# A two-block graph transformer on one core: maxima split on GpSimd, half of the masks there, q stored six times, new slots, and a last batch in the score banks

## The chip, the cores and the metric

The kernel runs on one core of one Trainium2 chip. The metric is the device time of one execution in microseconds, the median of several runs. TensorE (PE in the profile; PEld is its weight loading), VectorE (DVE), ScalarE (ACT), GpSimd (POOL) and SyncE (SP, which only issues DMAs here) each work through a queue of their own, in order, and wait for each other on semaphores.

## The reference, cut to what matters

```
x: (16, 512, 128)   adj: (512, 512) bool, symmetric, with the diagonal
h = relu(layernorm(x))
q, k, v = split(h @ W_qkv + b_qkv)                    # 8 heads of 16
attn = softmax(where(adj, q k^T / sqrt(16), -inf))    # per batch and head: 512 x 512
x = x + (attn v) @ W_out + b_out
h = relu(layernorm(x))
zl, zg, v = h @ Wl, h @ Wg, h @ Wv
A_l = max(cosine(zl, zl), 0),  A_g = exp(-|zg_i - zg_j|^2 / 2)   # both times adj, with the diagonal 0
K = 0.9 A_l / rowsum(A_l) + 0.1 A_g / rowsum(A_g)     # row sums floored at 1e-8
x = x + (K v) @ Wo
```

## The kernel before, in words

All 16 batches go through one software pipeline. Time is counted in **slots**, 32 to a batch. In slot u of a batch TensorE makes one 128x512 tile of scores (`scores`, L595; 8 heads x 4 row tiles), and VectorE adds the mask and reduces its row maxima in one instruction (L820). 21 slots later (`LAG`) TensorE makes the same scores a second time, turned (`turned_scores`, L608 and L609): keys on partitions, queries along the free axis. This product has 96 rows of q and k and three more, which subtract the maximum. ScalarE takes the exp (L979). Every four slots `attend` (L623) multiplies four tiles by v.

**Exactness.** q and k are split into three bf16 parts (hi, mid, lo), and the six important products of parts are six groups of 16 rows (`Q_PARTS`, `K_PARTS`): 96 rows. To get there, the parts are stored to DRAM (`split_dram`, L441, six DMAs of 128 KB: from SBUF's 128 partitions, 8 heads outermost in the destination) and loaded again in row order for each half of the heads (L410: six DMAs per half, three of them for q broadcasts of one stored part). The maxima of a half are split in three bf16 parts on VectorE (`max_split`, L828 to L835), turned on TensorE (`max_turn`, L689), copied by ScalarE (L1004) and loaded as three rows (L426). Other products split their float32 operands in two parts and make three matmuls (`split_product`, L630).

**Masks.** A turned tile is masked in one of two ways: TensorE adds a mask matrix to the bank ahead of the scores (L608; for w % 4 in `MASK_BY_PE` = 1, 2, 3, 24 tiles per batch), or GpSimd multiplies the exp's result by an integer mask (L485, the other 8), one slot after.

**The second block** of a batch works in the slots 62 to 99 after its first score, so beside the next two batches' attention. ScalarE copies z = h W (`z_copy`) and sums its squares (`z_sums`, L1057). GpSimd makes the norms (`z_norms`, L551 to L562) and divides zl by them. TensorE turns zg, zl and a bias (L641), makes four 128x512 tiles of the cosine and four of the rbf adjacency in one bank each (`adj_bank`), VectorE masks them (L843, L852, L857), and `mix` (L635) multiplies them by v. VectorE divides by the row sums (`out`, L863 to L874). The transposes, q, k, v, the maxima and the projection share one PSUM bank, `work_bank`; before a stage writes it, TensorE waits for the reader of the stage before (`bank_free`, `BANK_READ`).

**What sets the order** is the table `AT`: for each stage its slots counted from the first score of its batch. Every engine runs the same loop over slots and issues what `due` says is due, within a slot in the order in which the code has it. The slots set only the order in each queue; times follow from the waits. A stage at slot 78 of batch b stands in the queue where batch b + 2 is in its slot 14. `rows` and `qk_store` are negative: -16 is slot 16 of the batch before.

```
    "ln_rstd": (-33,), "q_split": (-24,), "k_split": (-18,), "x_biased": (-13,), "ln2_rstd": (61,),
    "qk_store": (-16,), "rows": (-11, -9), "x_next": (-14,), "max_load": (17, 33), "store": (98,),
```

The set-up turns the adjacency into masks on TensorE, ScalarE and VectorE, and GpSimd fills 32 rows of `qk_rows` with ones (L546, 6.9 us).

Of the kernel before, what the change touches and what calls it, by code (L numbers as in the profile page):

```python
# [5 lines left out]
F32 = mybir.dt.float32  # L6
F32R = mybir.dt.float32r
BF16 = mybir.dt.bfloat16
# [4 lines left out]
P = 128  # L13
# [7 lines left out]

Q_PARTS = (0, 0, 0, 1, 1, 2)
K_PARTS = (0, 1, 2, 0, 1, 0)
Q_RUNS = ((0, 3), (1, 2), (2, 1))
# [8 lines left out]
MASK_BY_PE = (1, 2, 3)  # L33
# [4 lines left out]
    "hT": (-26,), "q": (-24,), "k": (-22,), "v": (-15,), "max_turn": (16, 32),  # L38
    "pv": (28, 32, 36, 40, 44, 48, 52, 56), "y": (54, 59), "yT": (61,), "attn": (62,), "h2T": (67,),
    "z": (69, 70, 72, 73), "zgT": (76,), "col": (78,), "zlT": (79,), "rbf": (79, 83, 85, 87),  # L40
    "cos": (81, 83, 87, 89), "mix_cos": (93, 94, 96, 98), "mix_rbf": (94, 95, 96, 98),

    "ln_scale": (-28,), "hT_copy": (-26,), "q_hi": (-24,), "k_hi": (-22,), "max_copy": (15, 32),
    "pv_copy": (40, 57), "yT_copy": (60,), "ln2_scale": (64,), "h2T_hi": (67,), "z_copy": (69, 70, 72, 74),
    "z_sums": (70, 73, 74, 75), "zgT_hi": (75,), "col_copy": (77,), "zlT_hi": (78,), "rbf_exp": (82, 83, 85, 87),

    "ln_moments": (-35,), "hT_split": (-26,), "q_rest": (-24,), "k_rest": (-21,), "v_add": (-13,),
    "max_split": (15, 32), "y_scale": (55, 60), "x1": (62,), "ln2_moments": (62,), "h2T_lo": (67,),
    "zgT_lo": (76,), "zlT_lo": (79,), "rbf_read": (79, 83, 85, 87), "cos_read": (81, 83, 87, 91),
# [8 lines left out]
LAST = max(max(at) for at in AT.values()) + 1  # L58
# [14 lines left out]
def graph_blocks(nc, x, adj, w_qkv, b_qkv, w_out, b_out, w_l, w_g, w_v, w_o, out):  # L73
# [10 lines left out]
    ZC = 3 * D + 2  # L84
# [4 lines left out]

    def due(slot, name):  # L90

        for nth, at in enumerate(AT[name]):
            batch, rest = divmod(slot - at, SLOTS)
            if rest == 0 and 0 <= batch < B:
                return batch, nth
        return None
# [7 lines left out]
    with ExitStack() as ctx:  # L104
# [25 lines left out]
        bar_bias = sb("bar_bias", [P, 1])  # L130
        table_warm = sb("table_warm", [P, T])
        degree_floor = sb("degree_floor", [P, 2])
# [46 lines left out]
        inv_norm = sb("inv_norm", [P, T])  # L179
        rbf_bias = sb("rbf_bias", [P, T])  # L180
        zl_unit = sb("zl_unit", [P, T, D])
# [16 lines left out]
        split_dram = nc.dram_tensor("split_dram", (2, 3, DH, H, N), BF16, kind="Internal").ap()  # L198
# [15 lines left out]
        s_row_ones = signal("setup_row_ones")  # L214
# [36 lines left out]
        split_stored = [signal(f"split_stored{which}", 3, 16) for which in range(2)]  # L251
        rows_loaded = [signal(f"rows_loaded{h}", len(Q_RUNS) + len(K_RUNS), 16) for h in range(GROUPS)]
# [41 lines left out]
        unit_ready = signal("unit_ready")  # L294
# [19 lines left out]
        out_stored = signal("out_stored", 1, 16)  # L314

# [784 lines left out]
```

## Time and profile before

| | us |
|---|---|
| median of three runs | 914.6 (914.2 to 916.01) |
| the profiled execution | 914.57 |
| its span, first to last instruction | 912.8 |
| TensorE busy | 829.5 |
| VectorE busy | 718.8 |
| ScalarE busy | 532.2 |
| GpSimd busy | 348.7 |

The span is one execution's, from its first to its last instruction; the execution's own time is 1.8 us more. Busy times are sums over instructions, and busy TensorE is modelled at the ends of matmuls. Some matmul records are missing from the trace (307 of the 384 mask matmuls are in it).

### The profile page before, as it was taken

What the parts mean: (1) busy time and instruction counts of PE and PEld (TensorE: products, weight loads), DVE (VectorE), ACT (ScalarE), POOL (GpSimd) and SP (SyncE); (2) the same over time, 40 slices, a digit from 0 to 9 for tenths busy, and PEclk for the clock granted to TensorE, in tenths of its full rate; (3) what the DMA queues carried; (4) which work ended last, traced back from release to release, by engine and by line L of the source; (5) the groups of instructions that cost most, each with busy time, mean ns of one, the idle gap of its engine ahead of it and who ended that gap; (6) DMA issues with size and microseconds to landing.
All of it is one profiled execution on the core that took longest, in us unless ns stands there. A gap on an engine that the chain in (4) does not pass through costs nothing.

```text
span 912.8 us, 15340 instructions
## 1 busy us (share of the span) xinstructions
PE 829.5 (91%) x4870; PEld 482.8 (53%) x4947; DVE 718.8 (79%) x2078; ACT 532.2 (58%) x1226; POOL 348.7 (38%) x415
## 2 busy tenths in 40 slices
PE   3388899999999999999999999999999999999976
PEld 2133346546464646546564655646465554646455
DVE  5677879797887978798887979788797879786434
ACT  4136675856556575755647585655657575565630
POOL 5334452533435352443534253353525244233210
PEclk9569999999999999999999999999999999999987
DMA  3231313130311213030211213031121303000000
GB/s 98 69 104 43 88 36 82 29 94 24 86 39 47 72 37 92 27 87 30 68 50 48 83 29 91 23 89 39 40 77 34 97 21 88 23 1 13 1 12 12
DMA packets 43423, 48.45 MB, mean 53 GB/s; under 512 B 6992, under 2 KB 37200, under 8 KB 43344
## 3 DMA queue, kind: packets, MB, share of 16 engines
q1 hardware_dynamic: 43344, 47.47, 19.1%
q8 instruction: 41, 0.67, 0.3%
q14 instruction: 38, 0.31, 0.1%
HBM read 30.28 MB, written 16.78 MB: 52 GB/s over the span
## 4 chain that ended last, share of the span: by engine, by line
PE 78%; DVE 11%; issue 4%; DMA 3%; ACT 2%; POOL 1%; SPq 1%; DVEq 0%; ACTq 0%; POOLq 0%
PE adj L630 13%; PE adj L635 12%; PE pv L623 12%; PE score L595 12%; PE turned L609 12%; PE turned L608 6%; PE work L641 5%; PE work L630 3%; DVE scrap L820 3%; DMA qk_rows<-split_dram 2%; PE work L712 1%; PE work L730 1%; DVE rbf_arg L852 1%; DVE zgT_parts L947 1%; DVE max_parts L828 1%
## 5 line engine op out<-in xcount | busy, mean ns | idle before, releaser
L820 DVE CUSTOM_DVE_ANT_0 scrap<-score,mask_add 128x512 f32<-128x512 f32 x512 | 337.8, 684 | 49.3 <-PE score L595 45.6
L979 ACT ACTIVATE probs_t<-turned 128x512 f32<-128x512 f32 x512 | 293.3, 595 | 130.3 <-PE turned L609 127.6
L485 POOL TENSOR_TENSOR probs_t<-probs_t,keep_t 128x512 int32<-128x512 int32 x128 | 170.3, 1331 | 258.9 <-ACT probs_t L979 258.9
L595 PE MATMUL score<-qk_rows 96*128 96x512 bf16 x512 | 202.0, 396 | 18.0 <-DMA qk_rows<-split_dram 14.4
L609 PE MATMUL turned<-qk_rows 99*128 99x512 bf16 x512 | 195.3, 381 | 6.4 <-DVE zgT_parts L947 1.9
L623 PE MATMUL pv<-probs_t,v_cols 128*32 128x512 f32 x1024 | 136.4, 605 | 0.0
L608 PE MATMUL turned<-bar_t,ident_b 128*128 128x512 bf16 x307 | 117.4, 382 | 7.3 <-ACT probs_t L979 7.3
L595 PEld LDWEIGHTS score<-qk_rows 96*128 96x128 bf16 x512 | 50.0, 98 | 127.4 <-issue 77.7
L1013 ACT ACTIVATE rbf_exp<-rbf_arg,rbf_bias 128x512 f32<-128x512 f32 x64 | 46.1, 721 | 65.4 <-DVE rbf_arg L852 65.4
L609 PEld LDWEIGHTS turned<-qk_rows 99*128 99x128 bf16 x512 | 50.6, 99 | 44.3 <-issue 1.0
L635 PEld LDWEIGHTS adj<-z,adj_cos 128*128 128x128 f32 x512 | 66.5, 190 | 11.7 <-DVE adj_cos L843 2.1
L630 PE MATMUL adj<-zlT_parts 128*128 128x512 f32 x192 | 68.5, 466 | 2.2 <-DVE zlT_parts L952 1.4
L635 PE MATMUL adj<-z,adj_cos 128*128 128x130 f32 x512 | 67.8, 275 | 2.4 <-DVE adj_cos L843 1.4
L635 PE MATMUL adj<-z,adj_rbf 128*128 128x130 f32 x512 | 67.4, 275 | 0.0
L635 PEld LDWEIGHTS adj<-z,adj_rbf 128*128 128x128 f32 x512 | 63.2, 191 | 2.1
L630 PE MATMUL adj<-zgT_parts 128*128 128x512 f32 x192 | 63.2, 439 | 0.8 <-DVE rbf_arg L852 0.8
L523 POOL TENSOR_SCALAR var_eps<-moments 128x4 f32<-128x4 f32 x16 | 3.9, 241 | 149.1 <-DVE moments L803 149.1
L843 DVE SCALAR_TENSOR_TENSOR adj_cos<-adj,mask_t 128x512 f32<-128x512 f32 x64 | 44.0, 688 | 14.6 <-PE adj L630 14.5
L608 PEld LDWEIGHTS turned<-bar_t,ident_b 128*128 128x128 bf16 x384 | 38.1, 99 | 31.3 <-ACT probs_t L979 18.5
L630 PE MATMUL adj<-wz_parts,h2T_parts 128*128 128x384 f32 x192 | 52.4, 386 | 1.4 <-DVE h2T_parts L942 1.4
L515 POOL CAST split<-resid 128x512 bf16<-128x512 f32 x31 | 19.0, 611 | 85.8 <-DVE resid L896 85.8
L852 DVE TENSOR_TENSOR rbf_arg<-adj,col_term 128x512 f32<-128x512 f32 x64 | 43.8, 684 | 7.6 <-PE adj L630 7.6
(123 smaller groups left out, 1206.7 us busy)
## 6 DMA issues: line engine op xcount, KB each, us to landing
split_dram<-split SPq DMA_DIRECT2D x96, 128.0 KB
qk_rows<-split_dram SPq DMA_DIRECT2D x64, 192.0 KB
qk_rows<-split_dram SPq DMA_DIRECT2D x64, 128.0 KB
x_sb<-in_x_dram SPq DMA_DIRECT2D x16, 256.0 KB, 2.9
qk_rows<-split_dram SPq DMA_DIRECT2D x64, 64.0 KB
out_dram<-out_sb SPq DMA_DIRECT2D x16, 256.0 KB, 2.3
qk_rows<-max_rows SPq DMA_DIRECT2D x96, 4.0 KB, 1.7
adj_sb<-in_adj_dram SPq DMA_DIRECT2D x1, 256.0 KB, 2.9
```

The lines of the kernel that those rows point to most:

```text
L485: pool.tensor_tensor(tile, tile, keep_t[:, w // HG % T, :], ALU.mult).then_inc(probs_masked.sem, 1)
L595: pe.matmul(score_bank[u % 2][:, :], qk_rows[0:ROWS, b % 2, 0, h, t * P:(t + 1) * P], qk_rows[0:ROWS, b % 2, 1, h, :], start=True, stop=Tr ...
L608: pe.matmul(turned_bank[w % 2][:, :], ident_b[:, :], bar_t[:, j, :], start=True, stop=False)
L609: pe.matmul(turned_bank[w % 2][:, :], qk_rows[0:ROWS + 3, b % 2, 1, h, j * P:(j + 1) * P], qk_rows[0:ROWS + 3, b % 2, 0, h, :], start=w no ...
L623: last = pe.matmul(pv_bank[32 * hl:32 * (hl + 1), :], v_cols[:, b % 3, j, g * HG + hl, :], probs_t[:, k % 4, hl, :], start=(j == 0), stop= ...
L630: last = pe.matmul(dst, left(a), right(c), start=(part == 0), stop=(part == 2))
L635: last = pe.matmul(adj_bank[n % 2][:, at:at + D + 2], adjacency[:, m, n * P:(n + 1) * P], z[:, m, 2 * D:ZC], start=(m == 0), stop=(m == T ...
L641: last = pe.transpose(work_bank[:, t * P:(t + 1) * P], src(t), ident[:, :])
L820: dve.tensor_tensor_reduce(scrap[:, u % 2, :], score_bank[u % 2][:, :], mask_add[:, u % T, :], -1.0, 3.0e38, ALU.add, ALU.min, neg_max[:, ...
L852: dve.tensor_tensor(rbf_arg[:, m % 2, :], adj_bank[1][:, :], col_term[:, :], ALU.add).then_inc(rbf_arg_ready.sem, 1)
L979: act.activation(probs_t[:, k % 4, w % HG, :], turned_bank[w % 2][:, :], ACT.Exp, scale=SCALE).then_inc(probs_ready.sem, 1)
L1013: act.activation(rbf_exp[:, m % 2, :], rbf_arg[:, m % 2, :], ACT.Exp, bias=rbf_bias[:, m:m + 1]).then_inc(rbf_exp_ready.sem, 1)
```

## The change

- **Masks.** `MASK_BY_PE` is (2, 3): TensorE adds the mask for 16 tiles a batch, GpSimd multiplies 16.
- **Maxima.** The four steps of `max_split` move from VectorE's queue to GpSimd's; half 0 is turned in slot 17.
- **h.** ScalarE writes the first part of hT straight from the bank, then the copy; VectorE takes the rest from the bank too, without its cast (L884).
- **q and k.** q is stored six times, one for each group of rows, k three times: nine DMAs per batch; each half loads q in one DMA and k in three. The fill of ones is made by ScalarE in four activations.
- **Second block.** zl is turned without being divided; v is divided by the norm instead (`v_cos`), and the floor of the degree is scaled by it. z products wait for the second part of h only at their third matmul. A row of z has one column of constants, 129 columns are mixed for 130.
- **Idle matmuls.** 20 at set-up, and one in each of the slots 0 to 20, write a bank that nobody reads then.
- **Slots.** `AT` has new numbers throughout. Batches 14 and 15 have tables of their own (`AT_BEFORE_LAST`, `AT_LAST`). Batch 15 uses the four score and turned banks for z and for mixing, and `pv_bank` and `work_bank` as second banks of the cosine and rbf tiles; its squares are summed on VectorE; each row block is mixed into all four banks as it comes; the output is made step by step over four blocks and stored in four DMAs.

```diff
-MASK_BY_PE = (1, 2, 3)
+MASK_BY_PE = (2, 3)
+IDLE_SET_UP = 20
+IDLE_FIRST_SLOTS = range(0, LAG)
...
-    "qk_store": (-16,), "rows": (-11, -9), "x_next": (-14,), "max_load": (17, 33), "store": (98,),
+    "qk_store": (-12,), "rows": (-6, -4), "x_next": (-9,), "max_load": (-2, 29), "store": (95,),
...
+                            if which:
+                                places = [k_dram[part]]
+                            else:
+                                places = [q_dram[c] for c, p in enumerate(Q_PARTS) if p == part]
+                            for place in places:
+                                sp.dma_start(place.rearrange("f h n -> h f n"),
+                                             split[:, which, part, :]).then_inc(split_stored[which].sem, 16)
...
+                sp.dma_start(qk_rows[0:ROWS, batch % 2, 0, heads, :],
+                             q_dram[:, :, heads, :].rearrange("c f h n -> (c f) (h n)")
...
+                if hit := due(s, "max_split"):
+                    b, g = hit
+                    reached(pool, max_ready, b, (g + 1) * HALF)
+                    reached(pool, max_turned, b - 1, g + 1)
+                    pool.tensor_copy(max_parts[:, g, 0, :], neg_max[:, g, :]).then_inc(max_hi.sem, 1)
...
+                pe.wait_ge(s_mask_add.sem, 1)
+
+                reached(pe, hi_ready, 0, 2)
+                reached(pe, rest_ready, 0, 2)
+                idle(IDLE_SET_UP)
...
-                    reached(act, hT_split, b - 1)
+                    reached(act, qk_filled, b - 1)
+                    act.copy(hT_parts[:, 0, :], work_bank[:, :]).then_inc(hT_hi.sem, 1)
                     act.copy(hT[:, :], work_bank[:, :]).then_inc(hT_ready.sem, 1)
...
+                    pool.tensor_tensor(v_cos[:, :, 0:D], z[:, :, 2 * D:3 * D],
+                                       v_cos[:, :, D:D + 1].broadcast_to([P, T, D]),
+                                       ALU.mult).then_inc(v_cos_ready.sem, 1)
...
+        def z_bank(batch, t):
+            return (score_bank + turned_bank)[t] if batch == B - 1 else adj_bank[t % 2]
+        def cos_bank(batch, m):
+            return pv_bank if batch == B - 1 and m % 2 else adj_bank[0]
+        def rbf_bank(batch, m):
+            return work_bank if batch == B - 1 and m % 2 else adj_bank[1]
+        def mix_bank(batch, n):
+            return (score_bank + turned_bank)[n] if batch == B - 1 else adj_bank[n % 2]
```

**GpSimd's queue, one middle batch, slots 8 to 20.** `probs_t` rows are masks, `split` rows the parts of q and then k, `norm_floor` to the row with `z` the norms. Before:

```order
L515 CAST split<-resid 128x512 [waits rest_ready,split_stored0]
L517 TENSOR_TENSOR split<-resid,split 128x512 [waits mid_ready]
L485 TENSOR_TENSOR probs_t<-probs_t,keep_t 128x512 [waits probs_ready]
L551 TENSOR_SCALAR norm_floor<-square_sum 128x4 [waits sums_ready]
L555 TENSOR_SCALAR rbf_bias<-square_sum 128x4 [waits col_filled,rbf_exp_ready]
L558 TENSOR_TENSOR inv_norm<-norm_floor,minus_half 128x4 [waits floor_ready]
L562 TENSOR_TENSOR zl_unit<-z,inv_norm 128x512 [waits zlT_filled,inv_norm_ready]
L485 TENSOR_TENSOR probs_t<-probs_t,keep_t 128x512 [waits probs_ready]
L515 CAST split<-resid 128x512 [waits rest_ready,split_stored1]
L517 TENSOR_TENSOR split<-resid,split 128x512 [waits mid_ready]
L485 TENSOR_TENSOR probs_t<-probs_t,keep_t 128x512 [waits probs_ready]
```

and now:

```order
L625 TENSOR_SCALAR norm_floor<-square_sum 128x4
L629 TENSOR_TENSOR v_cos<-norm_floor,minus_half 128x4 [waits mix_filled,floor_ready]
L632 TENSOR_TENSOR v_cos<-z,v_cos 128x4x128 [waits inv_norm_ready]
L635 TENSOR_TENSOR norm<-norm_floor,v_cos 128x4
L639 TENSOR_SCALAR degree_floor<-norm 128x4 [waits out_ready,norm_ready]
L585 CAST max_parts<-neg_max 128x16 [waits max_turned,max_ready]
L587 TENSOR_TENSOR max_rest<-neg_max,max_parts 128x16 [waits max_hi]
L590 CAST max_parts<-max_rest 128x16 [waits max_rest_ready]
L592 TENSOR_TENSOR max_parts<-max_rest,max_parts 128x16 [waits max_mid]
L547 TENSOR_TENSOR probs_t<-probs_t,keep_t 128x512 [waits probs_ready] x4
L615 TENSOR_TENSOR x_resid<-x_sb,bias_out 128x512 [waits x1_ready,x_loaded]
L577 CAST split<-resid 128x512 [waits rest_ready,k_stored]
```

The four steps on `max_parts` now stand behind the norms and ahead of four masks, and the parts of k behind all of these.

**SyncE's queue from the maxima to the rows of the next batch's half 0.** Before:

```order
L453 DMA out_dram<-out_sb 128x4x128 [waits out_ready]
L441 DMA split_dram<-split 8x16x512 [waits hi_ready,rows_loaded1,rows_loaded0]
L441 DMA split_dram<-split 8x16x512 [waits hi_ready]
L441 DMA split_dram<-split 8x16x512 [waits mid_ready] x2
L441 DMA split_dram<-split 8x16x512 [waits lo_ready] x2
L426 DMA qk_rows<-max_rows 1x16x128 [waits turned_filled,max_copied]
L426 DMA qk_rows<-max_rows 1x16x128 x2
L377 DMA x_sb<-in_x_dram 128x4x128 [waits x_resid_ready,ln_done]
L410 DMA qk_rows<-split_dram 48x1x2048 [waits turned_filled,split_stored1,split_stored0]
L410 DMA qk_rows<-split_dram 48x2048
L410 DMA qk_rows<-split_dram 32x1x2048
```

and now, where the first six loads of maxima are half 1 of one batch and half 0 of the next:

```order
L477 DMA qk_rows<-max_rows 1x16x128 [waits turned_filled,max_copied]
L477 DMA qk_rows<-max_rows 1x16x128 x2
L510 DMA out_dram<-out_sb 128x4x128 [waits out_ready]
L497 DMA q_dram<-split 8x16x512 [waits hi_ready,rows_loaded1,rows_loaded0]
L497 DMA q_dram<-split 8x16x512 x2
L497 DMA k_dram<-split 8x16x512 [waits hi_ready]
L497 DMA q_dram<-split 8x16x512 [waits mid_ready]
L497 DMA q_dram<-split 8x16x512
L497 DMA k_dram<-split 8x16x512 [waits mid_ready]
L497 DMA q_dram<-split 8x16x512 [waits lo_ready]
L497 DMA k_dram<-split 8x16x512 [waits lo_ready]
L430 DMA x_sb<-in_x_dram 128x4x128 [waits x_resid_ready,ln_done]
```

The stores were ahead of the loads of half 0's maxima and are behind them now; after the last store only x stands ahead of the rows, whose first load (96x2048) follows it.

**TensorE's queue in the last batch, from z's transposes on.** Before, with one bank for each kind of tile and zl behind the bias:

```order
L641 MATMUL work<-ident,z 128x128 [waits h2T_split,z_ready]
L641 MATMUL work<-ident,z 128x128 x3
L641 MATMUL work<-ident,rbf_bias 128x128 [waits zgT_split,rbf_bias_ready]
L641 MATMUL work<-ident,rbf_bias 128x128 x3
L630 MATMUL adj<-zgT_parts 128x512 [waits z_ready,zgT_split]
L630 MATMUL adj<-zgT_parts 128x512 x2
L641 MATMUL work<-ident,zl_unit 128x128 [waits col_ready,unit_ready]
L641 MATMUL work<-ident,zl_unit 128x128 x3
L630 MATMUL adj<-zlT_parts 128x512 [waits z_ready,zlT_split]
L630 MATMUL adj<-zlT_parts 128x512 x2
L630 MATMUL adj<-zlT_parts 128x512 [waits cos_ready]
L630 MATMUL adj<-zlT_parts 128x512 x2
```

and now, with `pv` and `work` as second banks:

```order
L740 MATMUL work<-ident,z 128x128 [waits h2T_split,z_ready]
L740 MATMUL work<-ident,z 128x128 x3
L740 MATMUL pv<-ident,z 128x128 [waits pv_copied,z_ready]
L740 MATMUL pv<-ident,z 128x128 x3
L717 MATMUL adj<-zgT_parts 128x512 [waits out_ready,zgT_split]
L717 MATMUL adj<-zgT_parts 128x512 x2
L717 MATMUL adj<-zlT_parts 128x512 [waits out_ready,zlT_split]
L717 MATMUL adj<-zlT_parts 128x512 x2
L740 MATMUL work<-ident,rbf_bias 128x128 [waits zgT_split,rbf_bias_ready]
L740 MATMUL work<-ident,rbf_bias 128x128 x3
L717 MATMUL pv<-zlT_parts 128x512 x3
L717 MATMUL adj<-zlT_parts 128x512 [waits cos_ready]
```

The transposes of zl stand right behind those of zg and wait for no norm.

## Rows read from the trace of the kernel before

**Rows 1.** The page, busy shares and clock row.
```profile
PE 829.5 (91%) x4870; PEld 482.8 (53%) x4947; DVE 718.8 (79%) x2078; ACT 532.2 (58%) x1226; POOL 348.7 (38%) x415
...
PEclk9569999999999999999999999999999999999987
```

**Rows 2.** Windows: us, busy (x) PE, PEld, DVE, ACT, POOL, PEclk, DMA share, GB/s.
```profile
310.27:362.47 52.20, 50.02 (x305) 29.66 (x310) 44.03 (x130) 32.67 (x77) 21.13 (x25) 1.00 0.21 55
18.00:20.00 2.00, 0.00 (x0) 0.00 (x0) 2.00 (x3) 2.00 (x5) 2.00 (x2) 1.00 0.49 151
28.00:30.00 2.00, 0.00 (x0) 0.00 (x0) 1.66 (x9) 0.00 (x0) 0.16 (x1) 0.50 1.02 164
880.00:900.00 20.00, 14.24 (x41) 9.19 (x39) 7.79 (x12) 7.20 (x26) 2.50 (x4) 0.62 0.00 0
```

**Rows 3.** Timeline of TensorE in one middle batch.
```profile
314.33 0.38 PE L595 MATMUL score<-qk_rows 96*128 96x512 bf16 x1
...
342.54 0.22 PE L689 MATMUL work<-ident_b,max_parts 128*48 128x128 bf16 x1 [1.37 <-DVE zlT_parts L952]
...
353.69 0.38 PE L608 MATMUL turned<-bar_t,ident_b 128*128 128x512 bf16 x1
353.91 0.38 PE L609 MATMUL turned<-qk_rows 99*128 99x512 bf16 x1
```

**Rows 4.** Waits of TensorE, 310.27 to 362.47: us, times, longest.
```profile
PE work L689 <- DVE zlT_parts L952: 1.4, 1, 1.4
PE turned L608 <- ACT probs_t L979: 0.5, 1, 0.5
```

**Rows 5.** Groups by form: busy us, mean ns | idle before.
```profile
L820 DVE CUSTOM_DVE_ANT_0 scrap<-score,mask_add 128x512 f32<-128x512 f32 x512 | 337.8, 684 | 49.3 <-PE score L595 45.6
...
L1057 ACT ACTIVATE adj_cos<-z 128x128 f32<-128x128 f32 x128 | 38.9, 314 | 0.0
...
L835 DVE TENSOR_TENSOR max_parts<-max_rest,max_parts 128x16 bf16<-128x16 f32 x32 | 18.4, 574 | 1.1
...
L558 POOL TENSOR_TENSOR inv_norm<-norm_floor,minus_half 128x4 f32<-128x4 f32 x16 | 16.6, 1036 | 0.0
...
L1028 ACT COPY hT<-work 128x512 f32<-128x512 f32 x16 | 9.4, 585 | 8.5 <-PE work L641 8.5
...
L523 POOL TENSOR_SCALAR var_eps<-moments 128x4 f32<-128x4 f32 x16 | 3.9, 241 | 149.1 <-DVE moments L803 149.1
```

**Rows 6.** Single lines: min/median/max ns.
```profile
L857 DVE SCALAR_TENSOR_TENSOR adj_rbf<-rbf_exp,mask_t x64: 680/686/1190, 140.5 to 900.7; 128x512 f32<-128x512 f32 x64
...
L485 POOL TENSOR_TENSOR probs_t<-probs_t,keep_t x128: 1266/1277/1770, 59.7 to 856.1; 128x512 int32<-128x512 int32 x128
```

**Rows 7.** Timeline of SyncE's queue, start and middle.
```profile
15.41 4.22 SPq L441 DMA_DIRECT2D split_dram<-split  x6
...
319.03 1.82 SPq L426 DMA_DIRECT2D qk_rows<-max_rows  x3
```

**Rows 8.** The start: chain of work and TensorE's timeline.
```profile
19.07 3.21 DMA split_dram<-split
...
34.99 1.01 PE L595 MATMUL score<-qk_rows 96*128 96x512 bf16 x2 [12.57 <-DMA qk_rows<-split_dram]
...
53.23 0.30 PE L689 MATMUL work<-ident_b,max_parts 128*48 128x128 bf16 x1 [1.18 <-DVE max_parts L835]
...
69.43 0.38 PE L595 MATMUL score<-qk_rows 96*128 96x512 bf16 x1 [1.04 <-DVE neg_max L820]
...
89.61 0.24 PE L689 MATMUL work<-ident_b,max_parts 128*48 128x128 bf16 x1 [0.79 <-DVE max_parts L835]
...
107.69 0.39 PE L595 MATMUL score<-qk_rows 96*128 96x512 bf16 x1 [1.82 <-DMA qk_rows<-split_dram]
```

**Rows 9.** TensorE's timeline, the last batch.
```profile
888.57 1.65 PE L630 MATMUL adj<-zlT_parts 128*128 128x512 f32 x3 [1.40 <-DVE zlT_parts L952]
...
900.96 2.02 PE L635 MATMUL adj<-z,adj_cos 128*128 128x130 f32 x16 [1.38 <-DVE adj_cos L843]
```

More of the change, by code:

```diff
@@ L88, in graph_blocks, with slots_of @@
     by_pool = [w for w in range(SLOTS) if w % HG not in MASK_BY_PE]
-    def due(slot, name):
[L92 to L96, printed above, removed]
+    def slots_of(name, batch):
+        table = {B - 1: AT_LAST, B - 2: AT_BEFORE_LAST}.get(batch, AT)
+        return [at + SLOTS * batch for at in table.get(name, AT[name])]
+    stages = {}
+    for name in AT:
+        for batch in range(B):
+            for nth, at in enumerate(slots_of(name, batch)):
+                assert (at, name) not in stages
+                stages[at, name] = batch, nth
+    def due(slot, name):
+        return stages.get((slot, name))
     def tile_due(slot, lag):
@@ L568, in _, with idle @@
             pe.wait_ge(s_ident.sem, 1)
+            def idle(times):
+                for _ in range(times):
+                    pe.matmul(pv_bank[:, :], ident_b[:, :], mask_add[:, 0, :], start=True, stop=True)
             def turn_masks(blocks):
@@ L626, in attend, with split_product, mix, v_of_cos @@
                 last.then_inc(pv_filled.sem, 1)
-            def split_product(dst, left, right):
+            def split_product(dst, left, right, before_rest=None):
                 for part, (a, c) in enumerate(((0, 0), (0, 1), (1, 0))):
+                    if part == 2 and before_rest:
+                        before_rest()
                     last = pe.matmul(dst, left(a), right(c), start=(part == 0), stop=(part == 2))
                 return last
-            def mix(n, at, adjacency):
-                for m in range(T):
-                    last = pe.matmul(adj_bank[n % 2][:, at:at + D + 2], adjacency[:, m, n * P:(n + 1) * P],
-                                     z[:, m, 2 * D:ZC], start=(m == 0), stop=(m == T - 1))
-                return last
-            def turn_tiles(src, ready):
+            def mix(bank_, adjacency, n, right, rows):
+                for m in rows:
+                    last = pe.matmul(bank_, adjacency[:, m, n * P:(n + 1) * P], right(m), start=(m == 0),
+                                     stop=(m == T - 1))
+                return last
+            def v_of_cos(m):
+                return v_cos[:, m, :]
+            def v_of_rbf(m):
+                return z[:, m, 2 * D:ZC]
+            def cos_half(batch, n):
+                return mix_bank(batch, n)[:, 0:D + 1]
+            def rbf_half(batch, n):
+                return mix_bank(batch, n)[:, 256:256 + D + 1]
+            def turn_tiles(src, ready, bank_=work_bank):
                 for t in range(T):
-                    last = pe.transpose(work_bank[:, t * P:(t + 1) * P], src(t), ident[:, :])
+                    last = pe.transpose(bank_[:, t * P:(t + 1) * P], src(t), ident[:, :])
                 last.then_inc(ready.sem, 1)
@@ L868, in _ @@
[L868 to L875 removed]
+                    blocks = [n] if b < B - 1 else range(T)
@@ L959, in _, with fill_ones @@
             act.activation(table_warm[:, :], minus_half[:, :], ACT.Exp)
+            def fill_ones():
+                act.wait_ge(s_mask_add.sem, 1)
+                for half in range(GROUPS):
+                    for place in range(2):
+                        act.activation(qk_rows[ROWS:P, place, 1, half * HG:(half + 1) * HG, :],
+                                       mask_add[ROWS:P, :, :], ACT.Identity, bias=one[ROWS:P, 0:1],
+                                       scale=0.0).then_inc(s_row_ones.sem, 1)
             def cast_masks():
```

307 lines of the change are left out of this document (186 added, 121 removed).

## Prediction

> **What bounds the kernel now.** First the page's busy shares: TensorE 91% of the span, next VectorE 79% [rows 1]. A share is a mean over stages, so I cut one period out of the middle, 310.27 to 362.47, 52.2 us from a mixing step to the same one a batch later. In it TensorE is busy 50.0 us, VectorE 44.0, ScalarE 32.7, GpSimd 21.1 [rows 2]. Ends of matmuls are modelled, so I checked by starts: from a mask matmul's start to the next one's, 353.69 to 353.91, is 0.22 us [rows 3], and that is the distance nearly everywhere. What is left are two waits, 1.4 us before the transposed maxima (TensorE needs the work bank, which VectorE frees late) and 0.5 us behind ScalarE's exp [rows 4]. So the middle is bound by TensorE. The ends are not: the first score starts at 34.99, after 12.6 us of waiting for the rows of q and k [rows 8]; the clock row stands at half until 62 us and dips again near the end [rows 1]; and at the end the last batch runs alone through a chain of small steps, its first cosine product at 888.57 and its mixing from 900.96 [rows 9].
>
> **The middle: 13 batches (2 to 14).** Eight of the 24 mask matmuls per batch go: 8 x 0.22 = 1.76 us, all on the path, since TensorE is packed. GpSimd gets eight more masks of 1.28 us (10.2 us, from the median in [rows 6]), the eight small steps of the maxima (0.24 us each, 1.9 us) and two small ones in place of none [rows 5]: 21.1 + 10.2 + 1.9 + 0.5 = 33.7 of 50 us. A pair's masks are due four or more slots later (6 us) and take 2.6, so they lie beside other work. Of small GpSimd steps there are two prices in the trace, 0.24 us (add, multiply) and 1.04 us (power) [rows 5]. No row shows a 16-element split on GpSimd; I take 0.24, since it is a cast and a subtraction like the nearest row, and keep 1.04 for the range.
>
> VectorE loses the split of the maxima (its last step alone 0.57 us, twice a batch [rows 5]) and the cast of h, so it has under 43 of 50 us to do: nothing directly. But the 1.4 us wait was just this: the split stood in slot 15 ahead of the step that frees the bank [rows 4]. With the split gone and the turn one slot later, it goes: 1.4 us. What is late next is ScalarE. Slots 4 to 11 are its densest (a layer norm, eight squares of 0.31 us and their read-outs [rows 5], the copies of z, q and k), and TensorE stalls 0.5 us behind it. There it gets one copy more (0.585 us [rows 5]) and TensorE arrives 0.44 us earlier (two mask matmuls less): +1.0 us. Sum per batch: -1.76 - 1.4 + 1.0 = -2.2, a period of 50.0 us, and 13 x 2.2 = **28.6 us**. Norms that multiply v and not zl, one column less in the mixing and the new slots otherwise I cost at nothing: they exchange like for like inside GpSimd's 16 idle us and TensorE's queue. A misplaced slot would show as a new wait, between 0 and 1.5 us per batch (the largest one here is 1.4).
>
> **GpSimd beside VectorE.** The mask of the second adjacency on VectorE reads two SBUF tiles; it takes 686 ns at the median and up to 1190 [rows 6], so at most 0.5 us each, 2 us per batch on an engine with 7 us to spare. I take nothing, and 2 us for the range. The Trainium skill (SBUF — State Buffer, "Who interferes with whom") says that a VectorE instruction with two SBUF inputs is blocked by a GpSimd one that reads SBUF, for the whole instruction. By it twice the masks mean twice the collisions, which speaks against the change; an estimate from it and the mask's length would be up to 1.28 us for each of four steps, 5 us per batch. The row's longest excess, 0.5 us, agrees in kind and is far smaller.
>
> **The rows of q and k.** Now q is stored six times, so nine stores per batch where there were six, and they start only after the maxima of half 0 are loaded (SyncE's queue: turn, three loads, the output's store, then the nine). Six stores took from 15.41 to their landing at 22.28 [rows 7, 8], 6.9 us for 0.79 MB; the busiest window shows 151 GB/s with 0.49 of 16 engines [rows 2], so 5.2 us of data and 1.7 of the rest. Nine: 7.8 + 1.7 = 9.5 us, though the queue issues them in 5.2. The loads of half 0 bring 0.79 MB; at 164 GB/s, seen with all engines busy [rows 2], 4.8 us, with 1.2 to land 6.0. Before, the loads of half 0 took from about 22.3 to 34.7, 12.4 us [rows 8]. The skill (DMA: Bandwidth & Descriptors, "Why a DMA increments its semaphore by 16 and not by 1") says that a transfer uses the largest number of engines, at most 16, that divides the outermost size of both sides: three or two for the old broadcasts, all for the new loads, but eight for every store. By this rule the trace agrees: 0.49 of 16 is eight.
> In the middle this loop is: first score to turn, 28.2 before [rows 3], less four mask matmuls (0.9) and the 1.4 wait, with ScalarE's 1.0 and one slot's score, turned score and cosine product (1.3): 28.2. Then copy 0.3, three loads 1.8 [rows 7], output store 0.4, stores 9.5, x 0.5, loads 6.0, and 1.4 for the bytes of x and output in the same engines: 48.1 us, against a period of 50.0. Hidden, with 1.9 us to spare.
>
> **The start.** Stores from 15.5: 25.0, then x 0.2, loads 6.0: first score at 31.2 in place of 34.99. GpSimd's long fill of ones (7 us) moves to ScalarE, which idles there. Twenty idle matmuls (at 0.43 us, half clock, 8.6 us) lie inside TensorE's wait for rows and end by 31. One more in each of the first 21 slots lies under VectorE's 0.70 us per score (0.684 and a read-out [rows 5]). They are to hold the clock; if not, TensorE needs two times 0.43 per slot, 0.16 more than VectorE, 3 us. But the loop binds here, since early slots are short: batch 0 reaches the turn in 17.4 us (18.2 before, 34.99 to 53.23 [rows 8], less 1.5 for the clock and the split, plus a slot of 0.7) and batch 1 in 19.7 (20.2 before, 69.43 to 89.61 [rows 8], less 0.9 for mask matmuls and 0.8 of waiting, plus a slot of 1.2); each adds 0.3 + 1.8 + 9.5 + 0.5 + 6.0. So 31.2 + 35.5 + 37.8 = 104.5 for batch 2's first score, before 107.69 [rows 8]: **3.2 us** (0 to 8, the upper end if stores overlap better).
>
> **The end.** After batch 15's first score 13 mask matmuls fewer: **2.9 us**. Then the lone batch. Its projection and h2T come 1.4 us sooner, as its turn of y no longer waits behind mixing. The products of z go to four banks, start on the first part of h, and the squares leave ScalarE, where they delayed the z copies and the cast behind them (eight, 0.31 us each and a read-out), while zl's transposes no longer wait for the norms on GpSimd. I get the first cosine product 5.7 us sooner than 888.57 [rows 9]. From there to the end of the span the old chain takes 24.2 us: single banks, all mixing after 900.96, four outputs in turn. The new one has two banks each, and mixes row by row: eight VectorE reads and four masks in 10.8 us, the last four products 0.9, the four outputs step by step 3.8, the store 2.4: 17.9, so 6.3 saved. These are full-clock numbers; the row shows 0.62 there [rows 2], so I give back 2.5. **9.5 us** (5 to 12).
>
> **Sum.** The profiled execution took 914.57 us (span 912.8, 1.8 around it; median of the runs 914.6). 28.6 + 3.2 + 2.9 + 9.5 = 44.2, so **870.4 us**.
>
> **The rivals.**
> *The loop of rows binds in every batch.* If its true length is over 50, TensorE waits at each first score. For it: a margin of 1.9 us on a sum of eight terms, and two waits for rows at the start [rows 8]. Against: in the middle no wait for rows is in the list today [rows 4], and the new loads spread better. At 51.1 us (my sum short by 3): 13 x 1.1 + 15.6 = 29.9, 884.7 us.
> *All waits vanish.* The slots fit, and ScalarE's wait goes too: 50.0 - 1.76 = 48.3, just above the loop: 13 x 3.9 + 15.6, 848.3 us. Against: ScalarE's dense stretch is still there.
> *GpSimd becomes the bound, and it is slower.* All is in one queue in order: at the upper prices (small steps 1.04, masks 1.77 [rows 6]) its sum is 33.7 + 6.4 + 7.8 = 48 us, and it must wait some 6 us for square sums and for the last reduction before each split, with masks, the k split and stores queued behind. A period of 54.0: 13 x 1.8 longer, less 15.6, 922.4 us. It decides from 53.4 us per batch. Against: both upper prices are rare in the trace.
> *No effect:* TensorE only seems packed and another bound holds the middle near 53. Spacing of 0.22 between starts speaks against it.
>
> **Chances.** Forecast (860 to 880) 0.62, loop of rows 0.22, no waits 0.09, GpSimd 0.05, no effect 0.02. Two ends of unknown costs (start 3 to 5, end 4, new waits up to 13 x 0.7) and most of the loop's case give 854 to 889. Faster by over 0.2% (what a measurement of this kernel can tell) 0.93, within it 0.02, slower 0.05.
>
> **What would show it.** Mask matmuls 256 in place of 384, mean start spacing in the middle 50.0 us; the wait of the transposed maxima on VectorE gone, the one on exp near 1.5; GpSimd near 34 us per batch with small casts of 0.24; stores of nine in about 9.5 us; no wait for rows after batch 2; first score near 31; clock 1.0 from about 30 us on; 18 us from the first cosine product of batch 15 to the end. A wait of score matmuls on the row loads in each batch would make the loop right, one of pv on GpSimd's masks the third rival.

## The result, and the profile after

| | before | after | forecast |
|---|---|---|---|
| median, us | 914.4 (912.8 to 916.0) | 875.67 (872.3 to 875.9) | 870.4 (854 to 889) |
| ratio, 95% interval | | 0.9568 (0.9539 to 0.9596) | 0.952 |
| span of the profiled execution | 912.8 | 870.6 | 868.6 |
| first score of batch 0 | 34.99 | 30.41 | 31.2 |
| first score of batch 2 | 107.69 | 103.71 | 104.5 |
| first score of batch 15 | 784.41 | 755.16 | |
| steady period (batches 3 to 14) | 52.23 | 50.14 | 50.0 |

The traced execution of after is the shortest of its four (span 870.6 at a mean clock of 0.988). The other three, without a trace, took 873.9 to 874.1 at 0.983 to 0.986, so what they lost is not seen, only that they had more half clock.

The page's shares (columns as in [rows 1]) and one steady period by windows (columns as in [rows 2]):

```profile
PE 814.5 (94%) x4860; PEld 467.4 (54%) x4860; DVE 674.6 (77%) x1950; ACT 544.3 (63%) x1230; POOL 532.0 (61%) x701
...
PEclk9899899999999999999999999999999999999999
```

```profile
60.00:64.00 4.00, 1.32 (x5) 0.44 (x6) 1.56 (x6) 0.60 (x1) 2.06 (x6) 0.67 0.99 251
64.00:68.00 4.00, 4.00 (x15) 0.76 (x14) 1.06 (x3) 0.75 (x2) 1.66 (x4) 0.50 0.30 65
100.00:104.00 4.00, 1.11 (x4) 0.34 (x5) 3.17 (x15) 0.60 (x1) 1.50 (x8) 0.79 1.00 247
104.00:108.00 4.00, 4.00 (x14) 0.75 (x13) 0.85 (x3) 0.69 (x3) 3.69 (x6) 0.50 0.42 89
303.88:354.06 50.18, 49.25 (x303) 28.86 (x300) 41.67 (x120) 33.19 (x77) 33.03 (x44) 1.00 0.25 67
840.00:860.00 20.00, 17.41 (x118) 15.44 (x118) 14.44 (x52) 7.69 (x15) 4.60 (x10) 1.00 0.05 14
```

In the period GpSimd is busy 33.0 us, as forecast (33.7). The clock is full at the end (0.62 there before [rows 2]), but at half, 1.2 GHz, from 61.3 to 68.3 and from 102.3 to 109.3. Ahead of the first stands a wait of 4.02 us behind VectorE, and at both a wait for rows (TensorE's timeline):

```profile
60.40 0.39 PE L680 MATMUL score<-qk_rows 96*128 96x512 bf16 x1 [4.02 <-DVE neg_max L955]
...
63.50 0.61 PE L680 MATMUL score<-qk_rows 96*128 96x512 bf16 x1 [2.28 <-DMA qk_rows<-k_dram]
...
103.71 0.61 PE L680 MATMUL score<-qk_rows 96*128 96x512 bf16 x1 [2.64 <-DMA qk_rows<-k_dram]
...
852.85 0.40 PE L717 MATMUL adj<-zlT_parts 128*128 128x512 f32 x1
```

The last line is batch 15's first cosine product, 17.75 us ahead of the end (forecast 17.9). The waits of TensorE in the steady period, 303.88 to 354.06 (us, times, longest):

```profile
PE turned L694 <- ACT probs_t L1126: 0.6, 1, 0.6
PE adj L717 <- DVE rbf_arg L983: 0.4, 1, 0.4
```

The wait of the turned maxima [rows 4] is gone. A new one stands at the bank of the rbf tile, behind VectorE. Why VectorE is late there is seen when its timeline and GpSimd's are laid side by side. After, VectorE, then GpSimd:

```profile
334.72 1.71 DVE L988 SCALAR_TENSOR_TENSOR adj_rbf<-rbf_exp,mask_t 128x512 f32<-128x512 f32 x1
...
337.56 1.12 DVE L988 SCALAR_TENSOR_TENSOR adj_rbf<-rbf_exp,mask_t 128x512 f32<-128x512 f32 x1
```
```profile
334.58 1.30 POOL L615 TENSOR_TENSOR x_resid<-x_sb,bias_out 128x512 f32<-128x512 f32 x1
335.81 1.09 POOL L577 CAST split<-resid 128x512 bf16<-128x512 f32 x1
336.98 1.16 POOL L579 TENSOR_TENSOR split<-resid,split 128x512 bf16<-128x512 f32 x1
```

L988 takes 0.686 us at the median. At 334.72 it begins just behind GpSimd's addition, which ends at 335.88, and ends at 336.43, 0.55 after that. At 337.56 it begins inside a subtraction that ends at 338.14, and ends at 338.68, 0.54 after it. So it stands until GpSimd's instruction is over. The period's other two have no GpSimd instruction beside them and take 0.68 and 0.69. GpSimd waits in its turn: its cast is 1.09 long at 335.81 and 0.62 at the median. The Trainium skill (SBUF — State Buffer, "Who interferes with whom") says that whichever of the two engines issues first has the shared access to SBUF for its whole instruction, and that a VectorE instruction with two inputs in SBUF needs it beside a GpSimd instruction that reads SBUF. The trace agrees: 1.71 and 1.12 us for 0.686. The mask of the cosine tile reads one input from PSUM, and never takes over 0.692 us in this trace.

**Where the time came from**, profiled executions: up to batch 2's first score 4.0 us; from there to batch 15's 25.3 (676.7 before, 651.4 after); from there to the end 13.0; together 42.2 before rounding.

### The profile page after: what moved, and what is told of

The parts are those of the page before. It is cut to its first block, busy times and chain, and to the rows that moved or that the text cites. A ratio compares the mean times of both kernels' runs of the same rounds, so it can differ in the third digit from the quotient of the medians.

```text
span 870.6 us, 15444 instructions
## 1 busy us (share of the span) xinstructions
PE 814.5 (94%) x4860; PEld 467.4 (54%) x4860; DVE 674.6 (77%) x1950; ACT 544.3 (63%) x1230; POOL 532.0 (61%) x701
## 4 chain that ended last, share of the span: by engine, by line
PE 54%; DVE 16%; POOL 11%; issue 7%; ACT 6%; DMA 3%; SPq 2%; POOLq 0%; DVEq 0%; ACTq 0%
PE adj L722 12%; PE pv L708 9%; PE score L680 7%; PE turned L694 7%; DVE scrap L955 6%; PE adj L717 6%; PE work L740 4%; PE turned L693 4%; POOL probs_t L547 3%; DVE adj_cos L974 3%; DVE adj_rbf L988 3%; DVE rbf_arg L983 2%; PE work L717 2%; POOL v_cos L632 2%; POOL v_cos L629 2%
## 5 line engine op out<-in xcount | busy, mean ns | idle before, releaser
L547 POOL TENSOR_TENSOR probs_t<-probs_t,keep_t 128x512 int32<-128x512 int32 x256 | 322.4, 1280 | 213.4 <-ACT probs_t L1126 213.1
L693 PE MATMUL turned<-bar_t,ident_b 128*128 128x512 bf16 x256 | 98.0, 383 | 0.7 <-ACT probs_t L1126 0.7
L722 PEld LDWEIGHTS adj<-v_cos,adj_cos 128*128 128x128 f32 x480 | 62.8, 191 | 8.8 <-DVE out_sb L1011 0.6
L717 PE MATMUL adj<-zlT_parts 128*128 128x512 f32 x186 | 64.3, 454 | 0.1
L988 DVE SCALAR_TENSOR_TENSOR adj_rbf<-rbf_exp,mask_t 128x512 f32<-128x512 f32 x64 | 63.0, 985 | 1.2 <-ACT rbf_exp L1160 1.2
L722 PE MATMUL adj<-v_cos,adj_cos 128*128 128x129 f32 x480 | 63.4, 274 | 0.4 <-DVE out_sb L1011 0.4
L722 PE MATMUL adj<-z,adj_rbf 128*128 128x129 f32 x480 | 63.2, 275 | 0.0
L1151 ACT COPY max_rows<-work 48x128 bf16<-48x128 bf16 x32 | 8.2, 258 | 86.2 <-PE work L815 86.2
L717 PEld LDWEIGHTS adj<-zgT_parts 128*128 128x128 f32 x186 | 33.9, 189 | 22.4 <-DVE rbf_arg L983 11.9
L708 PEld LDWEIGHTS pv<-probs_t,v_cols 128*32 128x32 f32 x1024 | 20.3, 108 | 45.8 <-issue 29.2
L974 DVE SCALAR_TENSOR_TENSOR adj_cos<-adj,mask_t 128x512 f32<-128x512 f32 x62 | 42.5, 686 | 2.3 <-PE adj L717 2.3
```

What stands on the lines that cost most here:

```text
L547: pool.tensor_tensor(tile, tile, keep_t[:, w // HG % T, :], ALU.mult).then_inc(probs_masked.sem, 1)
L693: pe.matmul(turned_bank[w % 2][:, :], ident_b[:, :], bar_t[:, j, :], start=True, stop=False)
L708: last = pe.matmul(pv_bank[32 * hl:32 * (hl + 1), :], v_cols[:, b % 3, j, g * HG + hl, :], probs_t[:, k % 4, hl, :], start=(j == 0), stop= ...
L717: last = pe.matmul(dst, left(a), right(c), start=(part == 0), stop=(part == 2))
L722: last = pe.matmul(bank_, adjacency[:, m, n * P:(n + 1) * P], right(m), start=(m == 0), stop=(m == T - 1))
L974: dve.scalar_tensor_tensor(adj_cos[:, m, :], cos_bank(b, m)[:, :], 0.0, mask_t[:, m, :], ALU.max, ALU.mult).then_inc(cos_ready.sem, 1)
```

## Experiments: how many masks on GpSimd

Three kernels are the one after with another number of masks on TensorE: (1, 2, 3) in m24_pe, shown here, (3,) in m8_pe, and none in m0_pe. One, before_m16, is the kernel before with the change's (2, 3) alone.

```diff
-MASK_BY_PE = (2, 3)
+MASK_BY_PE = (1, 2, 3)
```

> The changed kernel with eight masks per batch put back on TensorE (24 of 32 there). Mine, TensorE packed: each mask matmul is worth its start spacing of 0.22 us, so the steady period goes from 50.14 to 51.9 us and the time from 872.3 to about 896 (1.76 x 13.5 batches). Rival, something else sets 50.14 (GpSimd's queue, slots, VectorE): less than a third of that, period under 50.7 and time under 880. The mask on VectorE that runs beside GpSimd's masks (985 ns mean now, 772 before the change) should fall towards 772.

> The changed kernel with eight more masks per batch on GpSimd (24 there, 8 on TensorE). TensorE packed and nothing else: period 48.4, time 849. Rival, GpSimd's queue in order becomes late: its busy time is 33.0 + 10.2 = 43.3 of 48.4 us, so the parts of the maxima and the masks come late; period 50 to 52 and a time of 872 to 895, with waits of pv on GpSimd's masks or of the turned maxima on their last part. I hold the rival's lower half likelier: 868 to 880, since three of four tiles would then be masked in one stretch of 7.7 us every 12.

> The changed kernel with all 32 masks on GpSimd, none on TensorE. GpSimd's busy time would be 33.0 + 20.5 = 53.5 us per batch, above the 50.14 of now. If busy time binds: period at least 53.5, time at least 872.3 + 13 x 3.4 = 916, the third rival of the prediction made real. If TensorE alone counted: period 46.6, time 826. The VectorE mask beside it should rise above 985 ns at the mean.

> The kernel before with the masks of the change alone (16 on TensorE). Mine, the term for masks in the sum: 8 x 0.22 = 1.76 us per batch, so about 914.4 - 1.76 x 13.5 = 890.6 us, and the wait of the transposed maxima for the work bank stays at 1.4 or grows. Rival, TensorE only arrives earlier at that wait and at the one on exp: half the gain or less, 903 and over.

| masks on TensorE | kernel | time | ratio to before | period | GpSimd busy in it | mean of VectorE's mask, ns |
|---|---|---|---|---|---|---|
| 24 | after | 885.1 | 0.9661 (0.9627 to 0.9696) | 50.93 | 22.8 | 806 |
| 16 | after | 875.7 | 0.9568 (0.9539 to 0.9596) | 50.14 | 33.0 | 985 |
| 8 | after | 899.6 | 0.9816 (0.978 to 0.9851) | 52.3 | 43.7 | 1274 |
| 0 | after | 975.4 | 1.0642 (1.0597 to 1.0686) | 56.6 | 53.9 | 1421 |
| 24 | before | 914.4 | 1 | 52.23 | 21.1 | 772 |
| 16 | before | 924.7 | 1.0091 (1.0067 to 1.0115) | 52.9 | 31.1 | 773 |

(The periods of the irregular kernels are means over 11 batches; the 43.7 is from a period of 51.62.) **Eight masks were worth 0.79 us a period, not 1.76.** Both theories of the first run miss. Laying one steady period of TensorE of m24_pe beside one of after, instruction by instruction, tells why: at each of the eight places TensorE gains 0.22 us, and elsewhere it gives 0.97 back. The largest step, +0.72, is the first product of an rbf tile at 340.55; the rest are steps of 0.08 and 0.09 around the exp and at transposes. In m24_pe the wait for the rbf tile's bank is not there:

```profile
PE turned L693 <- ACT probs_t L1126: 0.5, 1, 0.5
```

The price of a mask matmul was right, but what stood behind it was not free. (m24_pe keeps the slots that were chosen for 16 masks; no others were tried for it.)

**With 8 or none on TensorE** it is slower than either of my theories had it (899.6 for at most 895, and 975.4 for 916 or more), and before GpSimd is full: at 8 it is busy 43.7 of 51.6 us. Its norms come late in its queue, behind the masks, and TensorE waits for them, in m8_pe 13 times over the whole kernel; with none pv waits for the masks themselves, in m0_pe:

```profile
PE work L740 <- POOL rbf_bias L623: 18.1, 13, 1.4
```
```profile
PE pv L708 <- POOL probs_t L547: 63.7, 55, 3.4
```

Part of both losses is the clock. In m8_pe a period at full clock takes 51.6 us, and one in which the granted clock falls to half for a few microseconds 52.9 to 53.3; in m0_pe it falls in nearly every period (mean clock 0.934, 0.988 after).

**The kernel before with the change's masks alone is 0.9% slower.** Neither theory foresaw that: the rival's 903 and over was half the gain or less, not a loss. In one period (267.04 to 319.08) TensorE wins 8 times 0.22 and gives back 1.6: the wait for the work bank grows from 1.37 to 2.00, and the product of q waits for the parts of h, for which VectorE and GpSimd have these rows:

```profile
279.34 1.50 DVE L884 CAST hT_parts<-hT 128x512 fp32r<-128x512 f32 x1 [0.98 <-ACT hT L1028]
```
```profile
278.05 2.51 POOL L485 TENSOR_TENSOR probs_t<-probs_t,keep_t 128x512 int32<-128x512 int32 x2 [1.31 <-ACT probs_t L979]
```

The same cast took 0.43 us in the kernel before. Every second period the granted clock also falls to half behind the 2.00 us wait (0.79 over 346 to 354), and that period is 53.7 us in place of 52.0:

```profile
319.08:372.76 53.68, 50.37 (x297) 29.64 (x300) 45.67 (x131) 32.43 (x76) 31.13 (x33) 0.97 0.19 55
...
346.00:354.00 8.00, 6.11 (x24) 4.44 (x25) 5.45 (x13) 2.93 (x6) 4.20 (x4) 0.79 0.17 51
```

So TensorE's own work fell and the time rose. At full clock the period is still 0.2 shorter than before (52.04 for 52.23); what makes the kernel slower is the half clock of every second one.

## Experiments: who is shut out, one place at a time

**The residual's bias in another slot.** One number of the table moves the addition at 334.58 out of the way:

```diff
-    "x_biased": (-13,)
+    "x_biased": (-24,)
```

> The changed kernel with GpSimd's addition of the residual's bias moved from slot 19 to slot 8 (out of the stretch in which VectorE makes two masks of the second adjacency at 1.71 and 1.12 us in place of 0.686). Theory, the two engines shut each other out of SBUF: with 1.3 us of GpSimd's work gone from there VectorE gains 0.5 to 1.4 us, the wait of TensorE for the rbf tile's bank (0.37, with 0.35 around it) goes, the period falls from 50.14 to 49.5 to 49.9 and the time by 3 to 8 us, to 865 to 870. Rival, the long masks of VectorE have another cause, or the wait hangs on something else: the period stays within 0.1.

Measured 863.84 us, ratio 0.9431 (0.941 to 0.9452), against 0.9568 for after: faster by 11.8 us by the medians, 8.4 by the two spans. The period is 49.40, 0.74 less. Laid beside after, the one step is −0.72 at the rbf product; its wait is gone. VectorE's masks there:

```profile
332.98 1.04 DVE L988 SCALAR_TENSOR_TENSOR adj_rbf<-rbf_exp,mask_t 128x512 f32<-128x512 f32 x1
335.15 0.68 DVE L988 SCALAR_TENSOR_TENSOR adj_rbf<-rbf_exp,mask_t 128x512 f32<-128x512 f32 x1
```
```profile
333.56 1.50 POOL L579 TENSOR_TENSOR split<-resid,split 128x512 bf16<-128x512 f32 x1
```

Their mean is 757 ns (985 after). The row of GpSimd shows the lock from the other side: a subtraction of 1.16 us takes 1.50 when VectorE came first. No operation was added or taken away, the one step is where VectorE's mask was long, and every long one here lies beside a GpSimd instruction: the lock is the cause. The run gave more than the theory's upper end (865 to 870). Against m24_pe's 50.93 the eight masks fewer on TensorE are now worth 1.53 us of the 1.76, though m24_pe was not run with the early bias.

**The parts of h from SBUF, as before the change.**

```diff
-                    act.copy(hT_parts[:, 0, :], work_bank[:, :]).then_inc(hT_hi.sem, 1)
...
-                    dve.tensor_tensor(hT_parts[:, 1, :], work_bank[:, :], hT_parts[:, 0, :].bitcast(F32),
+                    dve.tensor_copy(hT_parts[:, 0, :], hT[:, :]).then_inc(hT_hi.sem, 1)
+                    reached(dve, hT_hi, b)
+                    dve.tensor_tensor(hT_parts[:, 1, :], hT[:, :], hT_parts[:, 0, :].bitcast(F32),
```

> The changed kernel with the first part of h made as before the change: VectorE casts it from the SBUF copy of hT and subtracts from that copy, ScalarE makes one copy only. In the kernel before with 16 masks on GpSimd this cast took 1.50 us beside two masks, 0.43 without them. Theory, GpSimd shuts VectorE's SBUF-only instructions out: the cast meets the pair of masks that ends near slot 9 and is long, the product of q waits 0.4 to 0.9 us, the period rises to 50.5 to 51.0, the time to 880 to 887. Rival, the part was worth nothing, as the prediction's sum has it (ScalarE's extra copy even costs): period 50.14 or less, time 869 to 876.

Period 50.52, 0.38 longer, span 876.5 (870.6 after). By the medians it is 878.12, ratio 0.9599 (0.9571 to 0.9627), whose interval overlaps after's: the period tells it, as the theory had it (50.5 to 51.0), the time hardly (880 to 887 was too high). The long one is not the cast (0.61 at the mean) but the subtraction, now with two inputs in SBUF, beside a pair of masks that ends at 319.99:

```profile
L1025 DVE TENSOR_TENSOR hT_parts<-hT,hT_parts 128x512 fp32r<-128x512 f32 x16 | 24.5, 1531 | 0.5
```

It takes 0.69 from the bank, with one input there. So the edit that I costed at nothing is one that pays for the masks.

**The maxima's split back on VectorE** (the same four steps in its queue, slots 15 and 31 for 13 and 30).

> The changed kernel with the four steps of the maxima's split back on VectorE (slots 15 and 31, turns where they are now). They took 2.9 us per batch of VectorE before the change (47.2 us for 128 steps). Mine: VectorE then has 44.6 us and more of 50, stands at the split when GpSimd runs its masks, and the wait of the turned maxima and of the rbf tile's bank grow: period 51 to 51.6 in place of 50.14, time 885 to 893. Rival, VectorE has 8 idle us and absorbs it: period within 0.3 of 50.14, time 872 to 879.

Measured 871.88 us, ratio 0.9522 (0.9496 to 0.9549), period 50.01: the forecast of my theory falls and the rival's period holds, but not for the rival's reason. Laid beside after, TensorE loses 0.75 us in three steps (0.32, 0.30 and 0.13), at two cosine products and a score, where it waits for VectorE, and wins 0.73 at the rbf product, whose wait is gone as in `x_resid_early`. GpSimd's queue is four steps of 0.2 us shorter ahead of its masks, so the addition and the casts meet L988 at another point, and its mean falls to 790 ns. So VectorE did not absorb the split; two effects cancel. The steps cost VectorE 44.5 us over the kernel, 2.8 per batch, though each takes 0.17 us when nothing is beside it: they too are shut out. The last of them, in the middle of this run:

```profile
327.46 1.27 DVE L957 TENSOR_TENSOR max_parts<-max_rest,max_parts 128x16 bf16<-128x16 f32 x1
```

The wait of 1.4 us [rows 4] was already made by this, and the prediction read it as a matter of order alone. In the kernel before, the four steps stand just ahead of the one that frees the bank and take from 338.72 to 341.20 for 0.7 us of work; the last of them, with GpSimd's instruction beside it:

```profile
340.17 1.03 DVE L835 TENSOR_TENSOR max_parts<-max_rest,max_parts 128x16 bf16<-128x16 f32 x1
```
```profile
339.98 1.18 POOL L517 TENSOR_TENSOR split<-resid,split 128x512 bf16<-128x512 f32 x1
```

With the split on VectorE again the wait at the bank stays away, so the engine that splits is not all of it; what else of the change ended it (the turn a slot later, zl's transposes that no longer come behind the division on GpSimd) was not tried apart.

## Experiments: the start and the end

**More idle matmuls**, into an adjacency bank, at the waits ahead of batches 1 and 2:

```diff
+IDLE_AT_ROWS = {30: 16, 32: 10, 64: 12}
...
+                    pe.matmul(adj_bank[0][:, :], ident_b[:, :], mask_add[:, 0, :], start=True, stop=True)
...
+                idle_apart(IDLE_AT_ROWS.get(s, 0))
                 if hit := tile_due(s, 0):
                     scores(*hit)
```

> The changed kernel with 38 more idle matmuls, into an adjacency bank that is free there: 16 ahead of slot 30, 10 ahead of slot 32 and 12 ahead of slot 64, the three waits of 4.02, 2.28 and 2.64 us behind which the granted clock fell to half for 7.8 and 6.3 us. Mine: the clock stays at full over 60 to 109 us, and about 4 us are saved (half of 14 us at most 7, less what the loop of the rows hides): 868 to 870. Rival, the loop of rows sets the start at either clock: no change, 871 to 875.

Measured 870.48 (869.6 to 870.9), ratio 0.9503 (0.9483 to 0.9524), between the two theories. The clock is full from 30 us to the last microseconds; the same four stretches as above:

```profile
60.00:64.00 4.00, 3.27 (x16) 1.35 (x15) 2.64 (x13) 1.19 (x2) 1.03 (x5) 1.00 0.91 243
64.00:68.00 4.00, 3.86 (x21) 1.00 (x20) 1.80 (x5) 1.43 (x4) 2.81 (x6) 1.00 0.65 145
100.00:104.00 4.00, 3.27 (x19) 1.17 (x18) 2.35 (x12) 0.53 (x1) 2.49 (x9) 1.00 1.05 223
104.00:108.00 4.00, 2.77 (x18) 0.95 (x18) 1.66 (x6) 2.76 (x8) 2.90 (x6) 1.00 0.20 36
```

Batch 2 takes 48.21 us from its first score to batch 3's, against 49.77 after. By the spans the gain is 1.8 us, by the medians 5.2; the three longer runs of after have no trace, and no run of this kernel is long.

**No idle matmuls** (`IDLE_SET_UP = 0`, no first slots).

> The changed kernel without its idle matmuls (20 at set-up, one in each of the first 21 slots). Mine: the granted clock is half from 22 to past 50 us, and since VectorE's 0.70 us per score and the loop of the rows bind there, batch 0 reaches its first turn 0 to 3 us later: time 873 to 879. Rival, half clock binds TensorE through batch 0 and 1 as before the change (41 us at half): 5 us and more, 880 and over.

Measured 875.59, ratio 0.9566 (0.9538 to 0.9594): as after. The clock is at half from 21 to 57 us and again from 64.5 to 71.5, and the first turn comes at 48.60, 2.7 us later; batch 2 starts 2.4 us later, but at full clock, and takes 48.22 us. The 41 idle matmuls of the change give nothing that this measurement can tell: of the 2.4 us that they win up to batch 2, 1.5 are lost in batch 2, over whose start the clock falls in the changed kernel (102.3 to 109.3) and not here.

**The last two batches on the common table and banks.** `table = AT` for every batch, and every test for the last batch never true.

> The changed kernel without the tables and banks of its last two batches (they run on the table of all others, in the adjacency banks, squares on ScalarE, output in one store). Mine: the term of 9.5 us comes back, of which 6.4 after the first cosine product, and the clock dips again in the lone batch as it did before (0.62 from 880 to 900): time 882 to 887. Rival, most of the end's gain came from the fewer masks and an earlier projection, which stay: time 877 to 879.

Measured 885.02, ratio 0.9664 (0.9635 to 0.9693): 9.4 us over after (forecast term 9.5). By the spans it is 12.6: 1.5 before batch 15's first score and 11.1 behind it. The first cosine product of batch 15 comes at 860.05, and 23.1 us follow (17.75 after), 5.4 of the forecast 6.4; the clock is at half again from 854 to 867.

## Experiments: both improvements together, and four masks more on GpSimd

`early_and_idle` has the bias in slot 8 and the 38 idle matmuls. `twelve_on_pe` is that kernel with

```diff
-    by_pe = [w for w in range(SLOTS) if w % HG in MASK_BY_PE]
+    by_pe = [w for w in range(SLOTS) if w % 8 in (2, 3, 7)]
```

> Both single improvements in one kernel: the residual's bias at slot 8 and the 38 idle matmuls at the waits for rows. They act at different places (steady period 49.40 for 50.14; the clock between 60 and 113 us), so their gains should add: 863.8 - 5.2 = 859, 857 to 861. If they don't add, 862 to 864.

> The kernel of the line before with 12 masks per batch on TensorE and 20 on GpSimd, in place of 16 and 16 (mask on TensorE where the tile's number modulo 8 is 2, 3 or 7). TensorE loses four times 0.22, so up to 0.88 us per batch: period 48.5, time 847. Rival, which the 24 masks on GpSimd speak for (period 51.6 to 53): GpSimd, 38 us busy in order, gives its norms late and shuts VectorE out more often, and the period is 49.2 to 50.5, time 857 to 872. I hold the rival a little likelier.

The first takes 860.45 us (859.1 to 862.7), ratio 0.9405 (0.938 to 0.9429), the fastest kernel of the study, 15 us under after by the medians and 11.7 by the spans; single gains of 11.8 and 5.2 would give 858.6, so they add within the spread of the runs. The second takes 885.56, ratio 0.9691 (0.9657 to 0.9725), slower than either theory said. In every period TensorE waits 0.78 us for exp and then 1.40 for GpSimd's norms, and about there the clock falls, again in every second batch (periods 50.3 and 52.2 in turn); timeline and window:

```profile
379.83 0.39 PE L699 MATMUL turned<-qk_rows 99*128 99x512 bf16 x1 [0.78 <-ACT probs_t L1132]
381.62 1.12 PE L745 MATMUL work<-ident,rbf_bias 128*128 128x128 f32 x4 [1.40 <-POOL rbf_bias L624]
```
```profile
380.00:386.00 6.00, 4.60 (x18) 3.00 (x17) 1.92 (x7) 2.25 (x5) 5.36 (x13) 0.72 0.01 3
```

## Why the prediction was right, and where its steps failed

- **The bound** was right: TensorE is packed, 49.2 of 50.2 us. Mask matmuls cost 0.22 each where nothing waits.
- **Masks, 1.76 us per batch:** the term that failed. It measured 0.79 net. The step was "a pair's masks are due four or more slots later, so they lie beside other work", with VectorE's loss taken as nothing. The masks were in time (no matmul of pv waits for them in the steady period), but GpSimd's denser queue moved its addition and its casts beside VectorE's masks, and a VectorE instruction with all inputs in SBUF is locked out for as long as such a GpSimd instruction runs.
- **"ScalarE late, +1.0":** right in size by luck, wrong in place. Exp's wait rose from 0.52 to 0.56. Of the microsecond 0.72 was given back at the rbf tile's bank, behind VectorE.
- **The bank wait, −1.4:** it went, but with the split back on VectorE (`split_on_dve`) it stays away too, at 0.75 us in other places. What I took for a place in the queue was in part the lock: the last step's 574 ns, which I quoted, are a mean of 0.17 alone and up to 1.12 beside GpSimd.
- **GpSimd beside VectorE, "nothing, 2 us for the range":** I had the rule and the row (up to 1190 ns) and judged by the median. VectorE's spare time of 7 us did not help, since L988 stands just ahead of a read that TensorE waits for.
- **13 batches times 2.2:** two faults. The period fell by 2.09; and batch 2's was 49.91 already before the change, and 49.77 after, when half clock took what the masks gave. 28.6 was 25.3.
- **The start:** 4.0 for 3.2, with stores of 9.3 us (48.43 issue to 57.77) for 9.5. Missed: VectorE waits 3.77 us for x behind those stores, and so TensorE 4.02; the loop hides it, but the clock does not forgive it. "Clock 1.0 from 30 us" was wrong for 14 us. The loads of half 0 took 5.7 (57.77 to 63.46) for 6.0.
- **The end:** 13.0 for 12.4 (2.9 and 9.5). By `last_undone` the tables and banks of the last batches alone are worth 11.1 behind batch 15's first score, and all the rest only 1.9: the second term was too small and the first too large.
- **The loop of rows** is hidden in the middle. The last load is issued by 347.7, half 0's rows have all landed at 349.96, and batch 7 starts at 354.06. **GpSimd as the bound** is real only with more masks (`m8_pe`, `m0_pe`), and then through late norms before it is full.

The sum was 2.0 us too optimistic against the profiled execution: too much for the middle by 3.3, too little for start and end by 1.4 (rounded). Against the median it was 5.3; the 3.3 more lie in executions without a trace.

## What to carry to other kernels

Before work goes to GpSimd, list VectorE's instructions that read only SBUF, and look which of them stands just ahead of something the bound engine waits for; move one of the two, or let the operand come from PSUM. A mean far above an instruction's shortest time is the sign to look for. The price of an instruction on the bound engine is what its removal gives only until the next wait; lay one period of both kernels side by side, instruction by instruction, to see where it is given back. A wait of 2 us, or two of 0.8 and 1.4 close together, can cost more than themselves, by the clock.

## What was not expected of the hardware

- The lock between VectorE and GpSimd works both ways and whole instructions long: 0.686 became up to 1.74 on VectorE and 0.17 (16 elements) up to 1.27, 0.61 became 1.09 and 1.16 became 1.50 on GpSimd. A one-input cast from SBUF to SBUF is hit as well (0.43 to 1.50); L974 and L983, with one input in PSUM, were not.
- A TensorE that is over 90% busy in each period can still lose its clock: behind a wait of 2.00 us, and behind 0.78 and 1.40 with a few products between, each time in every second batch, though the waits are the same in all. Behind the 1.37 us of the kernel before it did not fall.
